# Splitting the dense weights once on TensorE, normalizing the gate and up input once, and taking GpSimd out of the dense part of a two-layer adaptive-norm MoE kernel

## The chip, the cores and the metric

The program runs on one core of a Trainium2 chip. The metric is the device time of one execution in microseconds. Three runs of the kernel before took 5500.07, 5501.99 and 5503.63 us, so the median is 5501.99 us.

## What is computed

The input x has 4 sequences of 1024 tokens with 1024 channels; a side input has the same shape; each sequence has a condition vector of 256 numbers. Two layers follow each other, and both begin with the same kind of bidirectional decayed scan over time:

```python
def _bi_wkv(r, k, v, w, u, time_emb):
    tf = sigmoid(sum(time_emb))
    decay = exp(-exp(w)) * (0.5 + 0.5 * tf)
    ek = exp(min(k, 30)); ekv = ek * v
    # nf, df: forward scans of ekv and ek; nb, db: backward scans
    euk = exp(min(u + k, 30))
    num = nf + nb - ekv + euk * v
    den = df + db - ek + euk
    return sigmoid(r) * (num / maximum(den, 1e-08)) * (0.8 + 0.2 * tf)

x = x + _L0_ffn_ref(_bi_wkv(x, side, side, ...))       # one 1024 x 1024 product, scale, bias
x = x + _L1_ffn_ref(_bi_wkv(x, side, side, ...))       # residual inside: RMS norm, then
#   routed: softmax over 32 experts, top 4, silu(h @ w1_gate) * (h @ w1_up) @ w2 for each
#   shared: silu(h @ sg) * (h @ su) @ sd, with sg, su, sd of 1024 x 1024
```

## The kernel before, in words

Matrix products run in fp32r on split operands: every operand is written as a high half (a rounded copy, ScalarE) and a low half (operand minus high half), and a product is three matmuls, high x high, high x low and low x high.

**Scan units.** The 4 x 8 channel blocks of 128 channels are 32 units (`unit(u, fill)` on each engine). In a unit VectorE computes both layers' scans of one block over 1024 tokens: four scans of a layer (L808, L812, L821, L829), each with a small edge factor (L810, L823), and a dozen elementwise operations of 128x1024. ScalarE supplies exponentials, logarithms (L574, L576) and the sigmoid of x. The results go to `gated_dram` and `ratio_dram`, and the side input and x of the next unit are loaded, all by the SyncE queue.

**Halves and steps.** The dense part works on 8 halves of 512 tokens (`HALVES`). A half has 32 steps. Each step is one `product`: 24 matmuls of 128x512 over one 128-column piece of 1024 weights rows (L1174). Steps 0 to 15 alternate between layer 0 (L products, `step_l`) and the down projection of the half before (D products, `step_d`); steps 16 to 31 alternate gate and up (`step_g`). Four PSUM banks hold products. In every step ScalarE makes the high half of the weight piece (L598) and GpSimd its low half (L212, `split_piece_lo`), with two slots for a piece, which SyncE loads two steps ahead (`load_piece`, 512 KB). The same pieces are split again in each of the 8 halves.

**Order of the work.** `with_halves` writes out the order on every engine. Units 0 to 6 run alone. Unit 7 carries the loading and splitting of the input of half 0, and each of the units 8 to 31 carries 8 steps: `fill(i)` calls stand at eight fixed places in a unit, so that four units go with a half (halves 0 to 5). Halves 6 and 7 run without units. All engines are in order, so a `fill` that waits holds up the unit behind it.

**Around the normalization.** For each of the 8 channel blocks o of a half VectorE computes `XL` (L1029), `C1` (L1015), `Z = C1 * norm_w` (L1022) and `RES` (L1037); ScalarE makes the sigmoid, the square `SQ` (L634) and the high half of Z (L632); GpSimd makes its low half (L245); TensorE's `by_token`, at step `step_l(o) + 2`, transposes Z for the rows that the experts will gather, accumulates the router logits (L1190) and the sum of squares (L1192). Gate and up are computed from the input that is not yet normalized. The factor R = 1/rms is known at step 17; it is applied afterwards to the gate (L981 on VectorE, `gate_scaled`), once more by GpSimd to the up side (`gate_r`, L218; `gate_silu`, L223), and to the logits. GpSimd also makes the low halves of the activations (L228) and of the layer input (L257).

**Routing and experts.** In half 7 VectorE ranks the experts (`route`, from step 21 on, ending with `entry_ready`, L960). GpSimd first fills `slots_dram` with empty entries (`empty_slots`, L493) and then puts 128 groups of entries there (`put_entries`, L472 to L477), SyncE reads them back, GpSimd gathers token rows, and the experts run: 32 experts, weights of 6 MB each (L1273, L1287). R of each token goes through the slots to the experts as a second column of `gains`.

Of the kernel before, what the change touches and what calls it, by code (L numbers as in the profile page):

```python
# [28 lines left out]
PIECES = 10  # L29

def step_l(o):
    return 0 if o == 0 else 2 * o - 1
# [15 lines left out]
def adaln_moe(nc, x_t, side_t, cond, w_all, u_all, lin_sb, norm_w, router_t, shared_w, expert_w, out):  # L50
# [8 lines left out]
    slots_dram = nc.dram_tensor("slots_dram", (SLOT_TILES * P, 4), i32).ap()  # L59

    ctx = ExitStack()
    with ctx:
# [3 lines left out]
        def sem(name):  # L66
# [5 lines left out]
        halves = sb("halves", 6 * OP + 4 * PIECE, f32r)  # L72
        chi, clo, zhi, zlo, ahi_s, alo_s = (halves[:, i * OP:(i + 1) * OP] for i in range(6))
        piece_hi, piece_lo = ([halves[:, 6 * OP + (2 * i + part) * PIECE:6 * OP + (2 * i + part + 1) * PIECE]
                               for i in range(2)] for part in range(2))
# [5 lines left out]
        SCAN = 9 * SEQ  # L81
        work = sb("work", SCAN + 2 * PIECE + OP + 13 * HALF)
        K, X, EK, EKV, W, F, G, H, N = (work[:, i * SEQ:(i + 1) * SEQ] for i in range(9))
        piece_in = [work[:, SCAN + i * PIECE:SCAN + (i + 1) * PIECE] for i in range(2)]
        RES = work[:, SCAN + 2 * PIECE:SCAN + 2 * PIECE + OP]
        part0 = SCAN + 2 * PIECE + OP
        XL0, XL1, C10, C11, RL, Z, SQ, ZS, RS, OV, R, T, SG = (
            work[:, part0 + i * HALF:part0 + (i + 1) * HALF] for i in range(13))
        XL, C1 = [XL0, XL1], [C10, C11]
# [6 lines left out]
        entry = work[:, part0:part0 + TT * TOPK * 4].bitcast(i32)  # L96
        where = work[:, part0 + HALF:part0 + HALF + TT * TOPK].bitcast(i32)
        slots = work[:, part0 + 2 * HALF:part0 + 2 * HALF + 4 * SLOT_TILES].bitcast(i32)


        RESET, LG, CAND, INCL = K, X, EK, H
# [6 lines left out]
        acc = sb("acc", TT * 33)  # L108
        rms = sb("rms", TT)

        GT = SLOT_TILES
        gains = acc[:, 0:2 * GT]
# [31 lines left out]
        for name in (  # L144
            "k_in x_in ramp consts_in cond_in kc ek ekv euk h_fwd h_edge h_bwd h_all den g_ln g_inv nf n_edge nb "
            "wv_done num newton1 newton2 sig_steps sig_x gated gated_raw ratio ratio_out gated_out "
            "piece_hi piece_lo product read_out rl_in cl_in c_hi c_lo sig1_steps sig1 c1 z sq z_hi z_lo res "
            "z_tr sums z_copy z_out mean r_ln r_exp newton_r r_set scaled l_tr l_acc silu_steps silu_sig g_r "
            "g_silu a_hi_s a_lo_s o_tr o_copy o_out prep prep_act masks rt rt_act rt_mask rt_pe cnt_copy "
# [11 lines left out]
        piece_sem = [sem(f"piece_in{i}") for i in range(2)]  # L161
# [11 lines left out]
        def wait(eng, name, value):  # L173

            if not (isinstance(value, int) and value <= 0):
                eng.wait_ge(s[name], value)

# [32 lines left out]
        def split_piece_lo(eng, h, k):  # L210
            eng.wait_ge(s["piece_hi"], h * STEPS + (k + 1))
            eng.tensor_tensor(piece_lo[k % 2], piece_in[k % 2], piece_hi[k % 2].bitcast(f32),  # L212
                               ALU.subtract).then_inc(s["piece_lo"], 1)

        def gate_r(eng, h, j):

            eng.wait_ge(s["silu_steps"], (h * CB + j) * 2 + 1)
            eng.tensor_tensor(T, T, R, ALU.mult).then_inc(s["g_r"], 1)  # L218

        def gate_silu(eng, h, j):  # L220
            eng.wait_ge(s["silu_sig"], h * CB + (j + 1))
            eng.wait_ge(s["g_r"], h * CB + (j + 1))
            eng.tensor_tensor(T, T, SG, ALU.mult).then_inc(s["g_silu"], 1)  # L223

        def split_act_lo(eng, h, j):
            eng.wait_ge(s["a_hi_s"], h * CB + (j + 1))
            part = slice(j * HALF, (j + 1) * HALF)
            eng.tensor_tensor(alo_s[:, part], OV, ahi_s[:, part].bitcast(f32), ALU.subtract).then_inc(s["a_lo_s"], 1)  # L228

        def low_halves(eng, h, i, first, prev, next_):  # L230


# [1133 lines left out]
```

## Time and profile before

| | us |
|---|---|
| median of 3 runs | 5501.99 |
| the profiled execution | 5515.08 |
| its span, first to last instruction | 5513.1 |
| TensorE busy in the span | 4469.8 |
| VectorE busy | 3139.4 |
| ScalarE busy | 1907.9 |
| GpSimd busy | 1923.7 |
| mean granted TensorE clock, share of full speed | 0.936 |

The span is cut by the program into three parts: units alone until about 360 us, dense steps until about 2600 us, and, after a stretch in which TensorE is idle, the experts. The busy share of an engine is to be read part by part.

### The profile page before, as it was taken

The numbers are of one execution on the slowest core, as the hardware profiler recorded it, in microseconds if no ns is written. First come the engines' busy times: TensorE is split into PE (matmuls) and PEld (weight loads), VectorE is DVE, ScalarE is ACT, GpSimd is POOL, SyncE is SP. The second block draws the span as 40 slices with busy tenths as digits, with TensorE's granted clock in tenths as the row PEclk, the third lists the DMA queues.
The fourth block names the chain that finished last, engine by engine and source line by source line (L and its number), as shares of the span: only waits on it lengthen the run. The fifth ranks groups of instructions, "written<-read, shape, count | busy, mean of one in ns | idle before, by whom it ended". The sixth has DMA issues, their size and how long they took to land.

```text
span 5513.1 us, 61940 instructions
## 1 busy us (share of the span) xinstructions
PE 4469.8 (81%) x19471; PEld 3552.8 (64%) x19473; DVE 3139.4 (57%) x2812; ACT 1907.9 (35%) x2587; POOL 1923.7 (35%) x1350
## 2 busy tenths in 40 slices
PE   0036786868777787997459999999999999999998
PEld 0014555655555565765348888878878887888887
DVE  8889898988989896445222323434343214324232
ACT  2234444434444444442212223333343214223232
POOL 0023748475656657554721111111111111111111
PEclk9998888989888888998779999999999999999999
DMA  1123342424333334345433444545564435445352
GB/s 59 53 84 99 108 137 106 145 96 134 109 125 113 116 118 136 119 132 75 135 82 104 107 107 117 180 123 175 151 194 148 107 61 175 122 105 149 89 163 57
DMA packets 248186, 649.34 MB, mean 118 GB/s; under 512 B 44720, under 2 KB 110704, under 8 KB 223472
## 3 DMA queue, kind: packets, MB, share of 16 engines
q1 hardware_dynamic: 200224, 489.21, 26.0%
q0 software_dynamic: 47824, 158.43, 13.9%
q8 instruction: 69, 1.13, 0.1%
q14 instruction: 69, 0.57, 0.0%
HBM read 500.69 MB, written 146.87 MB: 117 GB/s over the span
## 4 chain that ended last, share of the span: by engine, by line
PE 53%; issue 2%; POOL 2%; DVE 1%; DMA 1%; ACT 0%; DVEq 0%; POOLq 0%; ACTq 0%; SPq 0%
PE ps L1273 30%; PE ps L1287 15%; PE ps L1174 4%; PE ps L1254 2%; POOL slots_dram L477 2%; PE ps L1262 1%; DMA slots_dram<-work 1%; PE ps L1192 0%; PE ps L1190 0%; DMA work<-slots_dram 0%; POOL halves L212 0%; DVE work L890 0%; DVE work L887 0%; DVE work L886 0%; POOL work L223 0%
## 5 line engine op out<-in xcount | busy, mean ns | idle before, releaser
L1174 PE MATMUL ps<-halves 128*128 128x512 f32 x6144 | 1606.3, 424 | 713.0 <-POOL halves L257 352.3
L1174 PEld LDWEIGHTS ps<-halves 128*128 128x128 f32 x6144 | 1249.5, 205 | 1066.7 <-issue 439.1
L1273 PE MATMUL ps<-halves 128*128 128x512 f32 x7152 | 1745.6, 397 | 27.5 <-DVE halves L1102 22.1
L1273 PEld LDWEIGHTS ps<-halves 128*128 128x128 f32 x7152 | 1328.9, 189 | 300.9 <-DVE halves L1102 24.3
L212 POOL TENSOR_TENSOR halves<-work,halves 128x1024 fp32r<-128x1024 f32 x239 | 694.9, 2909 | 675.7 <-ACT halves L598 675.4
L1287 PE MATMUL ps<-halves 128*128 128x512 f32 x3576 | 835.0, 389 | 1.3 <-DVE halves L1112 1.3
L1287 PEld LDWEIGHTS ps<-halves 128*128 128x128 f32 x3576 | 671.4, 188 | 140.5 <-DVE halves L1112 1.5
L1097 DVE TENSOR_TENSOR halves<-ps,halves 128x1024 fp32r<-128x1024 f32 x150 | 183.7, 1225 | 876.1 <-ACT halves L696 876.1
L459 POOL COPY add_idx<-work 128x1 int32 x149 | 27.0, 181 | 1692.1 <-DVE work L1118 1692.1
L1102 DVE TENSOR_TENSOR halves<-work,halves 128x1024 fp32r<-128x1024 f32 (+1 forms) x320 | 440.3, 1435 | 109.8 <-ACT halves L705 109.8
L696 ACT ACTIVATE halves<-ps 128x1024 fp32r<-128x1024 f32 x150 | 153.9, 1026 | 960.7 <-PE ps L1273 849.3
L705 ACT ACTIVATE halves<-work 128x1024 fp32r<-128x1024 f32 (+1 forms) x320 | 369.4, 1220 | 97.7 <-PE ps L1287 65.7
L598 ACT ACTIVATE halves<-work 128x1024 fp32r<-128x1024 f32 x256 | 268.3, 1048 | 271.8 <-PE ps L1174 167.2
L1107 DVE SCALAR_TENSOR_TENSOR work<-ps,acc,work 128x256 f32<-128x256 f32 x298 | 142.7, 479 | 285.1 <-ACT work L711 285.1
L462 POOL DMA_INDIRECT out<-work,add_idx x149 | 240.1, 1611 | 129.7 <-POOL add_idx L459 126.1
L1254 PE MATMUL ps<-ident,work 128*128 128x128 f32 x1200 | 156.2, 273 | 135.2 <-DMA work<-rows_dram,row_idx 135.2
L1118 DVE TENSOR_SCALAR work<-ps,acc 128x512 f32<-128x512 f32 x149 | 111.6, 749 | 266.1 <-PE ps L1287 259.5
L711 ACT ACTIVATE work<-ps,acc 128x256 f32<-128x256 f32 x298 | 140.2, 470 | 330.3 <-PE ps L1273 330.3
L257 POOL TENSOR_TENSOR halves<-work,halves 128x512 fp32r<-128x512 f32 x64 | 128.2, 2004 | 355.4 <-ACT halves L661 355.4
L1254 PEld LDWEIGHTS ps<-ident,work 128*128 128x128 f32 x1200 | 140.5, 140 | 154.7 <-DMA work<-rows_dram,row_idx 135.4
L1112 DVE TENSOR_TENSOR halves<-ps,halves 128x256 fp32r<-128x256 f32 x298 | 112.2, 419 | 220.2 <-ACT halves L716 220.2
L722 ACT ACTIVATE work<-ps,acc 128x512 f32<-128x512 f32 x149 | 101.3, 680 | 386.4 <-PE ps L1287 379.2
(163 smaller groups left out, 4582.0 us busy)
## 6 DMA issues: line engine op xcount, KB each, us to landing
work<-expert_w SPq DMA_DIRECT2D x192, 1024.0 KB, 5.5
work<-shared_w SPq DMA_DIRECT2D x256, 512.0 KB, 4.4
work<-side_t SPq DMA_DIRECT2D x33, 512.0 KB, 3.4
work<-x_t SPq DMA_DIRECT2D x33, 512.0 KB, 4.1
gated_dram<-work SPq DMA_DIRECT2D x32, 512.0 KB, 3.0
ratio_dram<-work SPq DMA_DIRECT2D x32, 512.0 KB, 2.9
work<-gated_dram SPq DMA_DIRECT2D x64, 256.0 KB, 2.7
work<-x_t SPq DMA_DIRECT2D x64, 256.0 KB, 3.2
```

Source lines behind the costliest of these rows:

```text
L212: eng.tensor_tensor(piece_lo[k % 2], piece_in[k % 2], piece_hi[k % 2].bitcast(f32), ALU.subtract).then_inc(s["piece_lo"], 1)
L462: pool.indirect_dma_start(out[:, :], bass.IndirectOffsetOnAxis(add_idx[:, :].bitcast(u32), 0), y, None, compute_op=ALU.add).then_inc(s["y_ ...
L598: sc.activation(piece_hi[k % 2], piece_in[k % 2], ACT.Copy).then_inc(s["piece_hi"], 1)
L696: sc.activation(xhi, ps_xt[:, :], ACT.Copy).then_inc(s["x_hi"], 1)
L705: sc.activation(whi[:, part], stage[:, part], ACT.Copy).then_inc(s["w_hi"], 1)
L1097: ve.tensor_tensor(xlo, ps_xt[:, :], xhi.bitcast(f32), ALU.subtract).then_inc(s["x_lo"], 1)
L1102: ve.tensor_tensor(wlo[:, part], stage[:, part], whi[:, part].bitcast(f32), ALU.subtract).then_inc(s["w_lo"], 1)
L1107: ve.scalar_tensor_tensor(part, ps_h[:, a * 512 + 256:a * 512 + 512], gains[:, ds(g + GT, 1)], part, ALU.mult, ALU.mult).then_inc(s["act_d ...
L1174: last = pe.matmul(bank(k % 4), w[k % 2][:, c * P:(c + 1) * P], op[:, part], start=(c == 0 and w is piece_hi and op is hi), stop=(c == CB ...
L1254: last = pe.transpose(ps_xt[:, c * P:(c + 1) * P], hx[:, c * P:(c + 1) * P], ident[:, :])
L1273: last = pe.matmul(ps_h[:, a * 512:a * 512 + 512], xp[:, xk * P:(xk + 1) * P], wp[:, rhs], start=(xk == 0 and xp is xhi and wp is whi), st ...
L1287: last = pe.matmul(ps_y[:, h * 512:h * 512 + 512], ap_[:, (q * 2 + k) * P:(q * 2 + k + 1) * P], wp[:, rhs:rhs + 512], start=(q == 0 and k ...
```

## The change

It is a set of edits that belong together.

1. **Weights are split once.** During the 8 first units, each of the 32 weight pieces is loaded into one of four raw buffers, ScalarE makes the high half, TensorE subtracts (identity times raw, plus negative identity times high, in fp32, into PSUM), ScalarE copies the difference as the low half, and SyncE stores both halves (1 MB) to `split_dram`. For the eighth unit's four pieces this is done ahead of the unit.
2. **Pieces are loaded already split.** A step loads 1 MB in two chunks of 512 KB, three steps ahead, in four slots. ScalarE's L598 and GpSimd's L212 are gone from the steps.
3. **The input of gate and up is normalized once**, in a burst at step 16. C1 of all 8 blocks is kept; Z = C1 * norm_w * R comes at step 16, block by block, with its two halves, transposes and logits. The sums of squares stay in the steps, at `step_l(o) + 1`. `gate_scaled`, `gate_r` and `gate_silu` become one VectorE multiply with the sigmoid; R no longer goes to the experts.
4. **GpSimd's remaining low halves move to VectorE** (8 for the layer input, 8 for Z, 8 for the activations in a half).
5. **In a unit** the two edge factors of a layer move from VectorE to ScalarE, both forward scans come first, and four operations change the buffer that they write.
6. Token rows are stored to `rows_dram` once a half (2 MB) and no longer block by block.
7. GpSimd waits for the last RES only before it fills `slots_dram`.

```diff
+        def alone(u, i):                       # SyncE
+            m = i // 2
+            if i % 2 == 0:
+                sp.wait_ge(s["split_pe"], u * 4 + (m + 1))
+                sp.dma_start(raw_w[m], shared_w[ds((u * 4 + m) * P, P), :]).then_inc(raw_sem[m], 16)
+            else:
+                sp.wait_ge(s["split_lo"], u * 4 + (m + 3))
+                sp.dma_start(split_dram[...], split_w[m]...).then_inc(split_sem[m], 16)
+        def alone(u, i):                       # ScalarE
+            m = i // 2
+            if i % 2 == 0:
+                sc.wait_ge(raw_sem[m], (u + 1) * 16)
+                sc.wait_ge(split_sem[m], u * 16 + 1)
+                sc.activation(split_part(m, 0), raw_w[m]..., ACT.Copy).then_inc(s["split_hi"], 1)
+            else:
+                sc.wait_ge(s["split_pe"], u * 4 + (m + 5))
+                sc.activation(split_part(m, 1), ps[m % 2]..., ACT.Copy).then_inc(s["split_lo"], 1)
+        with pe.Fori(0, 2 * UNITS_PER_HALF) as u:          # TensorE
+            for m in range(4):
+                pe.wait_ge(s["split_hi"], u * 4 + (m + 1))
+                pe.wait_ge(s["split_lo"], u * 4 + (m + 1))
+                for j in range(2):
+                    pe.matmul(ps[m % 2][:, part], ident[:, :], raw_w[m][:, part], start=True, stop=False)
+                    last = pe.matmul(ps[m % 2][:, part], neg_ident, split_w[m]..., start=False, stop=True)
+                last.then_inc(s["split_pe"], 1)
-            nothing = lambda i: None
             with eng.Fori(0, 2 * UNITS_PER_HALF - 1) as u:
-                unit(u, nothing, alone=True)
+                unit(u, lambda i: alone(u, i))
+            last = 2 * UNITS_PER_HALF - 1
+            for i in range(FILLS_PER_UNIT):
+                alone(last, i)
+            weights()
...
-                pe.wait_ge(s["piece_lo"], h * STEPS + (k + 1))
+                for j in range(2):
+                    pe.wait_ge(piece_sem[k % SLOTS][j], arrived(h, k))
...
-                    if i == step_l(o) + 2:
-                        by_token(h, o)
+                    if i == step_l(o) + 1:
+                        square_sums(h, o)
+                if i == 2 * CB - 1:
+                    for o in range(CB):
+                        by_token(h, o)
+                if i == 2 * CB:
+                    logits_by_token(h)
...
+        def normalize(h):                      # VectorE, at step 16
+            ve.tensor_scalar(SQ, SUM_BANK, 1.0 / CH, 1e-6, ALU.mult, ALU.add)
+            ve.wait_ge(s["r_exp"], h + 1)
+            ve.scalar_tensor_tensor(SG, R, -0.5, R, ALU.mult, ALU.mult)
+            ve.tensor_tensor(SG, SG, SQ, ALU.mult)
+            ve.scalar_tensor_tensor(R, SG, 1.5, R, ALU.add, ALU.mult)
+            for o in range(CB):
+                if o < 2:
+                    wait(ve, "l_tr", h)
+                else:
+                    ve.wait_ge(s["z_lo"], h * CB + (o - 1))
+                    ve.wait_ge(s["logits"], h * CB + (o - 1))
+                ve.scalar_tensor_tensor(Z[o % 2], C1[o], nrm[:, o:o + 1], R, ALU.mult, ALU.mult)
+                if o:
+                    split_z_lo(h, o - 1)
+            split_z_lo(h, CB - 1)
...
                     ve.tensor_tensor_scan(F, d, EK, 0.0, ALU.mult, ALU.add).then_inc(s["h_fwd"], 1)
+                    ve.tensor_tensor_scan(G, d, EKV, 0.0, ALU.mult, ALU.add).then_inc(s["nf"], 1)
-                    ve.tensor_scalar(edge_in[:, 0:1], F[:, SEQ - 1:SEQ], edge[:, at], None, ALU.mult)
-                    ve.tensor_tensor_scan(H[:, ::-1], d, F[:, ::-1], edge_in[:, 0:1], ALU.mult, ALU.add)
+                    ve.tensor_tensor_scan(F[:, ::-1], d, F[:, ::-1], edge_in[:, 0:1], ALU.mult, ALU.add)
```

## Rows read from the trace of the kernel before

**Rows 1.** The page: busy tenths in 40 equal slices of the span.
```profile
DVE  8889898988989896445222323434343214324232
...
POOL 0023748475656657554721111111111111111111
```

**Rows 2.** Windows: stretch, then length, PE, PEld, DVE, ACT, POOL busy (x count), PEclk, DMA share, GB/s.
```profile
811.00:973.00 162.00, 110.27 (x389) 85.43 (x388) 143.51 (x86) 67.73 (x86) 125.55 (x48) 0.82 0.28 99
973.00:1113.00 140.00, 118.63 (x481) 84.39 (x480) 127.68 (x95) 64.08 (x85) 63.67 (x24) 0.96 0.44 142
...
2811.00:5513.00 2702.00, 2657.65 (x12524) 2205.40 (x12522) 951.64 (x1205) 827.77 (x1206) 444.89 (x598) 0.99 0.45 128
```

**Rows 3.** VectorE's groups in 30 to 330 us, units alone, GpSimd idle.
```profile
L808 DVE TENSOR_TENSOR_SCAN work<-decay,work 128x1024 f32<-128x1024 f32 x14 | 32.0, 2284 | 0.0
...
L847 DVE SCALAR_TENSOR_TENSOR work<-work,neg_gain 128x1024 f32<-128x1024 f32 x14 | 18.0, 1284 | 1.1
```

**Rows 4.** VectorE's groups in 440 to 2050 us, units with steps, GpSimd busy.
```profile
L808 DVE TENSOR_TENSOR_SCAN work<-decay,work 128x1024 f32<-128x1024 f32 x43 | 127.9, 2976 | 0.0
L847 DVE SCALAR_TENSOR_TENSOR work<-work,neg_gain 128x1024 f32<-128x1024 f32 x43 | 121.3, 2822 | 5.2 <-DVE work L844 2.5
...
L991 DVE TENSOR_TENSOR work<-ps,work 128x512 f32<-128x512 f32 x41 | 28.1, 686 | 40.9 <-POOL work L223 40.9
```

**Rows 5.** VectorE's timeline: start, duration, line; two unit starts, an edge factor's place.
```profile
59.93 1.22 DVE L802 TENSOR_TENSOR work<-work 128x1024 f32<-128x1024 f32 x1
...
80.97 2.28 DVE L808 TENSOR_TENSOR_SCAN work<-decay,work 128x1024 f32<-128x1024 f32 x1
...
83.63 2.35 DVE L812 TENSOR_TENSOR_SCAN work<-decay,edge_in,work 128x1024 f32<-128x1024 f32 x1
...
102.18 1.22 DVE L802 TENSOR_TENSOR work<-work 128x1024 f32<-128x1024 f32 x1
```

**Rows 6.** VectorE's timeline: the start of unit 8 and the last operation of unit 31.
```profile
362.53 2.29 DVE L802 TENSOR_TENSOR work<-work 128x1024 f32<-128x1024 f32 x1
...
2151.51 2.19 DVE L847 SCALAR_TENSOR_TENSOR work<-work,neg_gain 128x1024 f32<-128x1024 f32 x1
```

**Rows 7.** TensorE's timeline: fp32 matmuls after an idle stretch and in dense work.
```profile
425.32 1.92 PE L1190 MATMUL ps<-work,rw 128*32 128x512 f32 x2
427.16 2.08 PE L1192 MATMUL ps<-work,ones 128*128 128x512 f32 x2
...
2181.73 1.05 PE L1190 MATMUL ps<-work,rw 128*32 128x512 f32 x2
2182.71 1.13 PE L1192 MATMUL ps<-work,ones 128*128 128x512 f32 x2
```

**Rows 8.** The chain that ended last: start, duration; two pairs of products in half 6.
```profile
2197.67 10.93 PE ps L1174 x48
2211.50 10.93 PE ps L1174 x48
```

**Rows 9.** DMA issues in 20 to 300 us: count, KB each, median us to landing.
```profile
work<-x_t SPq DMA_DIRECT2D x7, 512.0 KB, 3.8
work<-side_t SPq DMA_DIRECT2D x6, 512.0 KB, 3.3
```

**Rows 10.** ScalarE's groups over the span: a 128x1024 copy, a 128x512 square.
```profile
L598 ACT ACTIVATE halves<-work 128x1024 fp32r<-128x1024 f32 x256 | 268.3, 1048 | 271.8 <-PE ps L1174 167.2 <-DMA work<-shared_w 99.4 <-issue 5.2
...
L634 ACT ACTIVATE work<-work 128x512 f32<-128x512 f32 x64 | 39.3, 614 | 0.0
```

**Rows 11.** Timeline: the mean of squares in halves 6 and 7, `entry_ready`, the first put.
```profile
2267.93 0.68 DVE L1041 TENSOR_SCALAR work<-ps 128x512 f32<-128x512 f32 x1
...
2495.14 0.68 DVE L1041 TENSOR_SCALAR work<-ps 128x512 f32<-128x512 f32 x1
...
2564.70 0.09 DVE L960 MEMSET work<- 128x32 f32 x1
...
2588.68 0.18 POOL L472 COPY put_idx<-work 128x4 int32<-128x4 int32 x1 [26.79 <-DMA slots_dram<-work]
```

More of the change, by code:

```diff
@@ L29 @@
 PIECES = 10
+SLOTS = 4
+AHEAD = SLOTS - 1
 def step_l(o):
@@ L379, in store_out, with unit @@
                 sp.dma_start(to, RS.rearrange("p (t c) -> p t c", c=P)).then_inc(s["o_out"], 16)
-            def unit(u, fill, alone=False):
+            def unit(u, fill):
                 fill(0)
@@ L407, in _ @@
             load_x(0)
-            for k, src in first_half[:2]:
-                load_piece(0, k, src)
-            with_halves(sp, unit, fill, tail)
+            with_halves(sp, unit, fill, tail, alone, weights)
             def load_weights(j):
@@ L502, in fill @@
                     pool.dma_start(out[TOK:TOK + P, :], K).then_inc(s["y_out"], 16)
[L503 to L512 removed]
+            fill(HALVES - 2, 2, first=False, prev=True, next_=True)
+            fill(HALVES - 1, FIRST_RANK + 1, first=False, prev=True, next_=False)
             pool.wait_ge(s["entry_ready"], 1)
@@ L793, in clip, with unit @@
                 ve.tensor_scalar(EK, K, 30.0, None, ALU.min).then_inc(s["kc"], 1)
-            def unit(u, fill, alone=False):
+            def unit(u, fill):
                 fill(0)
@@ L1164, in product @@
+            pe.wait_ge(s["split_lo"], 2 * UNITS_PER_HALF * 4 + 2)
             def product(h, k, hi, lo, ready, at):
-                pe.wait_ge(s["piece_lo"], h * STEPS + (k + 1))
                 wait(pe, "read_out", h * STEPS + (k - 3))
-                for c in range(CB):
-                    if ready:
-                        pe.wait_ge(s[ready], at + (c + 1))
-                    part = slice(c * HALF, (c + 1) * HALF)
-                    for w, op in ((piece_hi, hi), (piece_hi, lo), (piece_lo, hi)):
-                        last = pe.matmul(bank(k % 4), w[k % 2][:, c * P:(c + 1) * P], op[:, part],
-                                         start=(c == 0 and w is piece_hi and op is hi), stop=(c == CB - 1 and w is piece_lo))
@@ L1176, in product @@
-                last.then_inc(s["product"], 1)
+                for j in range(2):
+                    pe.wait_ge(piece_sem[k % SLOTS][j], arrived(h, k))
+                    chunk = piece[k % SLOTS][j]
+                    for c in range(CB // 2 * j, CB // 2 * (j + 1)):
+                        if ready:
+                            pe.wait_ge(s[ready], at + (c + 1))
+                        part = slice(c * HALF, (c + 1) * HALF)
+                        col = c % (CB // 2) * P
+                        w_hi, w_lo = chunk[:, col:col + P], chunk[:, HALF + col:HALF + col + P]
+                        for w, op in ((w_hi, hi), (w_hi, lo), (w_lo, hi)):
+                            last = pe.matmul(bank(k % 4), w, op[:, part],
+                                             start=(c == 0 and w is w_hi and op is hi), stop=(c == CB - 1 and w is w_lo))
+                    last.then_inc(s["chunk" if j == 0 else "product"], 1)
@@ L1178, in by_token, with square_sums @@
+            def square_sums(h, o):
+                pe.wait_ge(s["sq"], h * CB + (o + 1))
+                if o == 0:
+                    wait(pe, "mean", h)
+                pe.matmul(SUM_BANK, ones[:, :], SQ, start=(o == 0), stop=(o == CB - 1)).then_inc(s["sums"], 1)
             def by_token(h, o):
```

532 lines of the change are left out of this document (258 added, 274 removed).

## The prediction, made before the changed kernel was run

> **What bounds the kernel now.** I read the page's slices first, then busy time by stretch, then VectorE's groups with and without GpSimd beside them, then the timelines. The slices [rows 1] show VectorE at 8 or 9 tenths until slice 15 or so, about 2100 us, and idle for the most part after. So the first 2150 us are VectorE's. From 2811 us on TensorE is busy 2657.7 of 2702 us [rows 2]; nothing in the change shortens that stage (the gate-up multiply loses a factor, but TensorE does not wait for it).
>
> The finding on which most hangs is that VectorE is not busy because it has so much to do. With GpSimd idle a forward scan takes 2.28 us, the last multiply 1.28 [rows 3]; with GpSimd busy the same lines take 2.98 and 2.82 [rows 4]. An operation that reads PSUM for one operand stays at 0.69 beside GpSimd [rows 4]. So what is slowed is work with both operands in SBUF, and GpSimd is what differs. Four units and 32 steps take 302 us in this stretch (162 + 140), of which VectorE is busy 271 [rows 2].
>
> **Part 1, the split during the units alone: a cost.** A unit alone takes 42.25 us (59.93 to 102.18 [rows 5]). The new work is a chain, and it is serial. SyncE is in order: it loads raw piece m, then waits for the low half of m before it stores it, and only then loads m + 1. Four raw buffers do not help. So every piece costs load, ScalarE copy, four fp32 matmuls, ScalarE copy.
> - Load: 512 KB alone lands in 3.3 us; x, issued right behind a 512 KB store, lands in 3.8 [rows 9]; with half a microsecond for the issue of the store, an estimate, 1 MB takes 4.3: so 2.3 us and 2 us per MB. In the same queue the four loads stand behind the 1 MB store of the last piece, and three of them also behind the unit's own transfers: 1.5, 2, 2.5 and 2 MB to be moved, so 5.3, 6.3, 7.3, 6.3: 25 us. Lower bound 3.3 each, upper 8.
> - Copies: 1.05 each [rows 10], two.
> - TensorE: one fp32 matmul of 512 columns takes 1.84 us start to start after an idle stretch (425.32 to 427.16) and 0.98 in dense work [rows 7]. The granted clock is at the lower of its two levels in the former, at the upper in the latter. TensorE idles some 8 us between pieces here, so I take the lower level for most: 6.3 us for four, between 3.9 and 7.4.
> - Hand-overs, four: 0.6 together, an estimate.
>
> A piece is then 9.0 us and its load, a unit 25 + 36 = 61 us, against VectorE's own 40.7, which is hidden in it. (VectorE's own: 42.25 less the edge factors, which take 83.63 - 80.97 - 2.28 = 0.38 us each, four of them [rows 5].) The Trainium skill, "DMA: Bandwidth & Descriptors", section on the anatomy of one DMA, puts a transfer at about 2.0 us and 436 GB/s. By it the four loads would take some 27 us, and the whole stage would be about 16 us longer; no run here shows a 1 MB store in front of a load.
>
> Seven units: 16 + 7 x 61 - 7 (the first has no store ahead) = 436. The eighth unit's pieces are split before it, with ScalarE and SyncE blocked, so VectorE waits: 4 x (5.3 + 9.0) = 57, until 493. Then SyncE waits for the last store (4.3), and issues six chunk loads ahead of the first layer input, which stands first in ScalarE's and VectorE's unit: 3.25 MB, 9 us; then its halves 1.4. Unit 7 starts at about 508 and takes 38.7 and 7 lows of 0.69: unit 8 starts at 552. Before: 362.5 [rows 6]. **Cost: 190 us.** Bounds: by the lower ends a unit is 44 us and the cost 60; by the upper ends (8 and 7.4) 72 us and 280.
>
> **Part 2, halves 0 to 5: the gain.** They take 362.5 to 2154 us, 1791, or 298.5 each. VectorE's work for a half without GpSimd: four units of 42.25 - 2 (the wait for the side input, hidden by steps here) - 1.5 = 38.7 make 155. Per block it now has ten operations of 0.69 (XL, C1, RES, down, Z, two gate multiplies, three lows): 55. With R's steps, 213. TensorE needs 32 x 5.47 [rows 8] and fp32 and transposes, about 206. Neither can be the time, because the new order ties them:
> - `square_sums(o)` stands one step earlier than `by_token` did. TensorE has just finished D, VectorE must add down (0.69), make C1 (0.69), ScalarE the square (0.61 [rows 10]) before the sum (1.0) and the next two products (10.9) and transposes (0.5): 14.7 us for a pair with hand-overs. VectorE's stretch between is longer in every other pair (two scans more): some 16.6 and 17.8. Steps 1 to 15 make 110 us.
> - At step 16 TensorE waits for everything: newton's start comes after down and RES, mean, two ScalarE operations, three on VectorE: Z0 is there 15 us after the last pair began; then 8 blocks of transposes and logits, with one PSUM bank for the transposes and two Z buffers: some 2.2 us each, and the first of them at the lower clock. 35 us in all, of which VectorE works 15.
> - Steps 16 to 31: VectorE has two units, 77.4, 15 or so multiplies and activation lows, 8 input lows (20.6 with them), stalls 4: 102. TensorE has 88 and is hidden. The next half's first stretch is 9.6.
>
> A half is 257 us. Half 0 has no D products: 235. Sum 1520. **Gain: 271 us.** Bounds for a half: 240, if the wait at each pair is hidden by the units, and 275, if every hand-over costs half a microsecond more. Weights come at 1 MB a step; three steps ahead is 16 us against some 5, so I cost it at nothing. If that cover is gone (SyncE held by a store that waits for VectorE), TensorE is late next.
>
> **Part 3, halves 6 and 7.** Between their means 227.2 us pass [rows 11]. A pair took 13.83 [rows 8], and 14.7 now, plus the burst of step 16, less the by-token work taken out of the pairs; in steps 16 to 31 GpSimd no longer slows anything: 230. Cost 3.
>
> **Part 4, routing.** From half 7's mean to the first put 93.6 us pass; 24 of them after `entry_ready`, waiting for the fill of `slots_dram` [rows 11]. Now the fill starts with the last RES, ahead of the burst and not after step 21, which is more than those 24 us earlier, so the puts start at `entry_ready`. From mean to `entry_ready` 69.6 us pass [rows 11]. The burst now stands in between: 24 us from mean to product 16, where before TensorE was in its products within 4; the copies of R that are gone give back 2.5. So 87. Gain 7.
>
> Sum: 190 - 271 + 3 - 7 = -85. Profiled execution 5515.1 - 85 = 5430; the median stands 13 us below that execution, so **5417 us**.
>
> **Costed at nothing.** The edge factors on ScalarE: the second forward scan and the backward one (2.3 us each) cover them and the exponential behind them; without that cover VectorE waits some 1 us in each layer. The logarithms now write the buffer whose store they wait for; that store was issued a scan or more earlier. Rows stored once a half (2 MB) instead of 8 times: SyncE issues 7 fewer, and the only ones who wait are ScalarE's first layer-input half at step 24, 15 us and more behind, and the gathers. The experts' silu without its scale: TensorE is busy 98% there [rows 2]. GpSimd's added mask: TensorE waits for it only at the start.
>
> **Rivals.**
> 1. *The split hides better*: TensorE stays at its upper clock and transfers overlap, 44 us a unit. For it: the queue's 2 MB are not one block. Against: SyncE's order. Then 130 us less: 5287. Chance 0.12.
> 2. *The lockstep eats the gain; slower.* Place: the pairs of steps 1 to 15 and the burst. In order engines wait for each other twice a pair, and each of four engines can be late with unit work. It decides from 257 + 85 / 6 = 271 us a half on. At 275 to 280, 1660 us for part 2: 5547. For it: VectorE idles 30 us a half even now. Against: a quarter of that is waiting for GpSimd (40.9 us at L991 alone in 5.4 halves [rows 4]). Chance 0.22.
> 3. *VectorE stays slow*, the slowing being due to transfers or ScalarE. Then nothing is gained in part 2, and the time is 5417 + 271 = 5688. ScalarE and transfers run beside the units alone too, at the undisturbed durations [rows 3]. Chance 0.03.
>
> **How the numbers follow.** The forecast keeps 0.63. The range takes in its unknowns: half of the way to both bounds in parts 1 and 2. 5310 reaches close to rival 1, 5550 holds most of rival 2. No change is within 0.2%, 11 us, about what a measurement of this kernel can tell. The forecast's 0.63 is 0.57 faster and 0.06 same; with rival 1 faster has 0.69. Of the 0.25 of rivals 2 and 3, 0.02 end within the bound: slower 0.23, same 0.08.
>
> **What would show it.** Unit starts in the first stage 61 us apart, VectorE waiting there for ScalarE, and ScalarE for the raw loads and TensorE. Unit 8 at about 550. Forward scans at 2.28 us, the last multiply at 1.28 in every part, GpSimd idle till the slots. Halves of 257 us, TensorE waiting for the square at each pair and about 6 us at step 16. Wrong if units alone stay near 42 us, or if halves are over 271 us.

## The result, and the profile after

The changed kernel takes **5607.46 us** (median; 5604.76 to 5610.94), the kernel before, beside it on the same chip, 5502.81. The ratio is 1.0191, with a 95% interval of 1.0173 to 1.0209: **1.9% slower**. The prediction of 5417 us, range 5310 to 5550, was wrong, and in its sign. The span went from 5513.1 to 5606.3 us, and these 93 us can be laid out by the events that the prediction used (starts and ends from VectorE's and GpSimd's timelines; the rows of before are [rows 6, 11]):

| stretch | before | after | difference | predicted |
|---|---|---|---|---|
| start to unit 8 (L802, now L832) | 362.5 | 573.8 | +211 | +190 |
| units 8 to 31, halves 0 to 5 | 1791 | 1679 | -112 | -271 |
| end of unit 31 to the mean of half 6 | 114 | 123 | +9 | 0 |
| mean of half 6 to mean of half 7 | 227.2 | 229.2 | +2 | +3 |
| mean of half 7 to the first put | 93.5 | 84.4 | -9 | -7 |
| first put to the end | 2924.4 | 2917.5 | -7 | 0 |

One row is wrong by 159 us, and the sign hangs on it. The windows of the changed kernel, cut at the stages (length, then busy us and count of TensorE, its weight loads, VectorE, ScalarE and GpSimd; granted clock, DMA share, GB/s):

```profile
16.00:444.00 428.00, 159.78 (x216) 61.56 (x216) 257.96 (x172) 129.16 (x149) 0.00 (x0) 0.67 0.37 132
444.00:574.00 130.00, 43.23 (x71) 20.14 (x72) 45.75 (x38) 29.51 (x35) 0.00 (x0) 0.62 0.32 113
574.00:2256.00 1682.00, 1292.70 (x4998) 966.24 (x4997) 1213.09 (x1103) 636.51 (x922) 0.76 (x1) 0.87 0.53 182
2256.00:2604.00 348.00, 302.91 (x1254) 231.92 (x1252) 106.63 (x147) 86.33 (x138) 0.00 (x0) 0.95 0.64 196
...
2905.00:5606.00 2701.00, 2656.30 (x12524) 2203.34 (x12524) 933.71 (x1205) 801.21 (x1206) 446.31 (x598) 0.99 0.45 128
```

The expert stage is as it was (2701 us, [rows 2] had 2702). In the dense part GpSimd is empty, and VectorE is now busy 1213 us of 1682, 72%, where the 302 us of [rows 2] had 90%. So the work did shrink. No engine is full: TensorE has 77%, and it is granted 0.87 of its clock. VectorE's groups in 900 to 2100 us show that the shrinking came as forecast:

```profile
L838 DVE TENSOR_TENSOR_SCAN work<-decay,work 128x1024 f32<-128x1024 f32 x34 | 77.6, 2283 | 0.0
L870 DVE SCALAR_TENSOR_TENSOR work<-work,neg_gain 128x1024 f32<-128x1024 f32 x34 | 43.7, 1285 | 2.8
```

These are the durations of [rows 3]; beside GpSimd they had been 2976 and 2822 ns [rows 4]. What is new is in the waits of the same stretch, 4.2 halves (us in total, times, longest):

```profile
PE ps L1223 <- ACT work L664: 151.0, 35, 13.9
...
DVE work L1078 <- PE ps L1215: 110.1, 28, 6.0
DVE halves L1025 <- ACT halves L697: 91.8, 32, 7.5
...
DVE work L1034 <- PE ps L1215: 64.9, 18, 7.2
```

L1223 is the matmul of `square_sums`; it waits for ScalarE's square of the block, at every block. L1025 is `split_c_lo`, the low half of the next layer input, now VectorE's. And VectorE waits for TensorE's products (L1215) while TensorE waits for it: a lockstep. TensorE's timeline (start, duration, line, idle before) shows one whole pair of it:

```profile
1447.68 1.54 PE L1223 MATMUL ps<-work,ones 128*128 128x512 f32 x2 [3.50 <-ACT work L664]
1448.24 7.66 PE L1215 MATMUL ps<-halves 128*128 128x512 f32 x24
1455.74 0.60 PE L1249 MATMUL ps<-ident,work 128*128 128x128 f32 x4
1456.10 5.74 PE L1215 MATMUL ps<-halves 128*128 128x512 f32 x24
1464.03 1.13 PE L1223 MATMUL ps<-work,ones 128*128 128x512 f32 x2 [2.20 <-ACT work L664]
```

Two things are to be seen. The wait: 2.20 us here, 2.04 or 2.20 in 20 of the 40 places between 700 and 2110 us, and 3.5 us or more in the others. And the product behind it: the same 24 matmuls take 7.66 us there and 5.74 in the second place. The windows over the product behind the second of these waits (it began at 1464.59 and took 7.66 us again) say why:

```profile
1466.00:1468.00 2.00, 2.00 (x6) 1.61 (x5) 1.96 (x2) 0.00 (x0) 0.00 (x0) 0.50 1.07 379
...
1470.00:1472.00 2.00, 2.00 (x10) 1.64 (x9) 0.00 (x0) 0.00 (x0) 0.00 (x0) 1.00 0.90 262
```

In the wait of 2.20 us that ends at 1464 the granted clock is still 1.00 (1462 to 1464 us); from 1466 on it stands at 0.50, the lower of its two levels, and it is back at 1.00 when this product nears its end. It is not so each time: of the 20 such products behind a wait of 2.0 to 2.2 us, 8 took 6.03 to 6.06 us and 12 took 7.03 to 7.67; the 20 behind a wait of 3.5 us or more took 6.99 to 8.45. So most waits cost themselves and some 1.6 us more.

The first pair of a half has the longest wait:

```profile
1396.26 8.36 PE L1215 MATMUL ps<-halves 128*128 128x512 f32 x27 [6.29 <-DVE halves L1025]
1418.48 2.07 PE L1223 MATMUL ps<-work,ones 128*128 128x512 f32 x2 [13.86 <-ACT work L664]
1419.56 8.30 PE L1215 MATMUL ps<-halves 128*128 128x512 f32 x24
```

ScalarE's sigmoid of block 0 stood behind the exponential and the sigmoid of a unit (it began at 1414.02), and VectorE's C1 behind a scan (at 1417.09).

### The profile page after: what moved, and what is told of

It reads as the page before. It is cut to its first block, busy times and chain, and to the rows that moved or that the text cites. A ratio compares the mean times of both kernels' runs of the same rounds, so it can differ in the third digit from the quotient of the medians.

```text
span 5606.3 us, 61272 instructions
## 1 busy us (share of the span) xinstructions
PE 4612.6 (82%) x19727; PEld 3603.9 (64%) x19729; DVE 2648.6 (47%) x2813; ACT 1737.9 (31%) x2531; POOL 599.8 (11%) x811
## 3 DMA queue, kind: packets, MB, share of 16 engines
q0 software_dynamic: 47824, 158.43, 13.5%
## 4 chain that ended last, share of the span: by engine, by line
PE 66%; DVE 12%; issue 8%; DMA 6%; ACT 5%; POOL 2%; SPq 1%; DVEq 0%; POOLq 0%; ACTq 0%
PE ps L1320 29%; PE ps L1334 14%; PE ps L1215 13%; DMA plain<-shared_w 3%; PE ps L1301 2%; PE ps L1223 2%; POOL slots_dram L494 1%; DMA work<-gated_dram 1%; PE ps L1195 1%; DVE work L853 1%; DVE work L838 1%; PE ps L1309 1%; DVE work L841 1%; DVE work L844 1%; PE ps L1196 1%
## 5 line engine op out<-in xcount | busy, mean ns | idle before, releaser
L1215 PE MATMUL ps<-halves 128*128 128x512 f32 x6144 | 1579.4, 418 | 165.9 <-DVE halves L1025 83.6
L1215 PEld LDWEIGHTS ps<-halves 128*128 128x128 f32 x6144 | 1229.4, 202 | 495.8 <-issue 151.9
L1195 PE MATMUL ps<-plain,ident 128*128 128x512 f32 x128 | 112.3, 975 | 321.1 <-ACT halves L626 321.1
L1223 PE MATMUL ps<-work,ones 128*128 128x512 f32 x128 | 99.2, 866 | 267.0 <-ACT work L664 267.0
L1195 PEld LDWEIGHTS ps<-plain,ident 128*128 128x128 f32 x128 | 35.5, 308 | 378.3 <-ACT halves L626 347.9
L1134 DVE TENSOR_TENSOR work<-ps,work 128x256 f32<-128x256 f32 x298 | 124.9, 419 | 240.9 <-ACT work L742 240.1
L1223 PEld LDWEIGHTS ps<-work,ones 128*128 128x128 f32 x128 | 24.2, 236 | 294.9 <-ACT work L664 294.8
```

The source lines that it names most:

```text
L1134: ve.tensor_tensor(part, ps_h[:, a * 512 + 256:a * 512 + 512], part, ALU.mult).then_inc(s["act_done"], 1)
L1195: pe.matmul(ps[m % 2][:, part], ident[:, :], raw_w[m][:, part], start=True, stop=False)
L1215: last = pe.matmul(bank(k % 4), w, op[:, part], start=(c == 0 and w is w_hi and op is hi), stop=(c == CB - 1 and w is w_lo))
L1223: pe.matmul(SUM_BANK, ones[:, :], SQ, start=(o == 0), stop=(o == CB - 1)).then_inc(s["sums"], 1)
```

## The experiments

The theory after these readings: the change lost by its order, in three places. (a) TensorE waits for each block's square, and loses clock by it. (b) VectorE waits for the upper halves of the input, where GpSimd used to wait. (c) The split is a chain of hand-overs, in which each load waits for the store of the piece before. The general rival: units and products set the pace anyway, and the waits only show it.

Each kernel ran with the kernel before beside it (medians of 5501.9 to 5510.1 us), and the ratio is to that.

| kernel | median, us | ratio to before, 95% interval | a half, us |
|---|---|---|---|
| changed | 5607.5 | 1.0173 to 1.0209 | 283.1 |
| e1 | 5348.8 | 0.9701 to 0.9733 | 246.4 |
| e2 | 5515.9 | 1.0014 to 1.0033 | 266.5 |
| e3 | 5436.5 | 0.9864 to 0.9897 | 282.4 |
| e4 | 5683.3 (one run) | | 306.0 with GpSimd busy |
| e5 | 5563.8 | 1.0093 to 1.0126 | 275.5 |
| e6 | 5496.6 | 0.9980 to 0.9999 | 265.1 |
| c1 | 5075.3 | 0.9195 to 0.9225 | 228.7 |
| c2 | 5046.0, again 5045.1 | 0.9158 to 0.9183 (the second) | 228.8 |
| c3 | 5021.9 | 0.9113 to 0.9138 | 227.2 |

A half is the distance from the mean of half 0 to that of half 5 (L1039 in VectorE's timeline), divided by five.

### e1: the square one product later

```diff
-                        if i == step_l(o) + 1:
+                        if i == step_l(o) + 2:
                             square_sums(h, o)
```

> Only the matmul that adds up the squares of a block moves, one product later in TensorE's order (the old order). Theory (lockstep): in the changed kernel TensorE waits 35 times, 151 us in 4.2 halves, for the square of the block that VectorE has only just finished, and after each such wait the granted clock drops and the next product takes 7.66 us and not 5.72. With the square one product later the square is 5 us old when TensorE comes to it: the waits of TensorE at L1223 go from 151 us to under 15, the products of the pairs are all near 5.7 us, a pair falls from 17.4 to 13.5 us, a half from 284 to 258 us (250 to 268) and the kernel from 5607 to about 5455 us (5400 to 5510), below the kernel before. Rival (VectorE and the work of the units are the bound anyway, TensorE's wait only shows their pace): the wait moves to another line, a half loses under 5 us, and the kernel stays above 5575 us.

Measured: 5348.8 us, 259 less than the changed kernel and 2.8% under the kernel before. The gain is larger than the theory's range. TensorE's timeline in e1:

```profile
1592.35 0.60 PE L1249 MATMUL ps<-ident,work 128*128 128x128 f32 x4
1592.79 1.02 PE L1223 MATMUL ps<-work,ones 128*128 128x512 f32 x2
1593.25 11.46 PE L1215 MATMUL ps<-halves 128*128 128x512 f32 x48
1604.55 0.60 PE L1249 MATMUL ps<-ident,work 128*128 128x128 f32 x4
1604.98 1.02 PE L1223 MATMUL ps<-work,ones 128*128 128x512 f32 x2
1605.44 11.47 PE L1215 MATMUL ps<-halves 128*128 128x512 f32 x48
```

A pair is 12.2 us (1592.79 to 1604.98), with no idle time in it and both products at 5.73. In the changed kernel the pair above took 16.35 (1447.68 to 1464.03), and those with the longer waits up to 19.9. The theory had 13.5. The waits at the squares in 900 to 2100 us, and what TensorE waits for now:

```profile
PE ps L1215 <- DVE work L1004: 62.5, 11, 7.8
PE ps L1233 <- DVE work L1055: 31.6, 5, 6.7
PE ps L1223 <- ACT work L664: 28.8, 9, 5.3
```

28.8 us are left, not under 15: at the first pair of a half and at one or two others. Of the five short ones between 690 and 1910 us, those of 1.31, 1.62 and 1.66 us left the two products behind them at 11.49 us; behind those of 1.73 and 1.74 us the granted clock fell to 0.50 again, and the two products took 12.98 and 13.06. The stretch without units gained as well: from the mean of half 6 to that of half 7 207.9 us pass and not 229.2, so it is not unit work alone that makes the square late. The rival is refuted: a VectorE that set the pace would have kept it.

### e5: useless matmuls in the wait

The square stays at its early place, and TensorE has something to do before it:

```diff
...
+                for n in range(9):
+                    pe.matmul(Z_BANK, chi[:, 0:P], chi[:, 0:HALF], start=True, stop=True)
                 pe.wait_ge(s["sq"], h * CB + (o + 1))
```

The lines left out let TensorE wait, before the first block, until the bank that the useless products write is free.

> The changed kernel, but before each wait for a square TensorE does nine matmuls of 128x128 by 128x512 in the halves' type, whose result nobody reads (nine of the 24 of a product of 5.74 us: 2.15 us of work, as long as its shortest waits). The square stays where it is. Theory (the lockstep costs twice: 2.2 to 3.5 us of wait, and then a product at a lower granted clock, 7.66 and not 5.74 us): with TensorE busy in the wait the first product of a pair takes 5.7 to 6.2 us, a pair falls from 17.4 to about 15.6 us, a half loses 9 to 14 us although TensorE has 17 us more to do in it, and the kernel comes to 5515 to 5560 us. Rival 1 (the clock falls for another reason, or the longer product is only what the wait's end makes of it): the first product stays at 7.66 us, the kernel within 5595 to 5620 us. Rival 2 (the added matmuls lie on the path): the kernel is slower, 5640 to 5720 us.

Measured: 5563.8 us. With 17.6 us more work for TensorE in each half (nine matmuls in 2.20 us, eight times), the kernel is 44 us **faster**. The timeline:

```profile
1475.18 2.20 PE L1224 MATMUL ps<-halves 128*128 128x512 f32 x9
1477.55 1.13 PE L1228 MATMUL ps<-work,ones 128*128 128x512 f32 x2 [0.16 <-ACT work L664]
1478.11 6.03 PE L1215 MATMUL ps<-halves 128*128 128x512 f32 x24
...
1460.25 2.07 PE L1228 MATMUL ps<-work,ones 128*128 128x512 f32 x2 [3.71 <-ACT work L664]
1461.34 8.11 PE L1215 MATMUL ps<-halves 128*128 128x512 f32 x24
```

Where the filling leaves 1.5 us of wait or less, all 30 first products take 6.02 to 6.06 us (granted clock 1.00 in 1478 to 1484 us); where it leaves 3.7 us or more, all ten take 6.95 to 8.32 (0.50 in 1461 to 1465 us). So the clock's part is real and separate: the square comes by the same path, and only what TensorE did meanwhile differs. A half lost 7.6 us, under the theory's 9 to 14, and the kernel missed the range by 4 us; the ten longer waits are those that outlast the filling. Of the 36.7 us a half that e1 wins, at least these 7.6 are the clock.

### e2 and e6: who waits for the input halves

e2 moves `load_cl` ahead of `next_piece` (and the loads of the first two of the eight blocks a step earlier), and puts ScalarE's copy first in the step:

```diff
+                if next_:
+                    for c in range(CB):
+                        if i == STEPS - CB + (c - 1 if c > 1 else 0 if before_all(h) else -1):
+                            load_cl(h + 1, c)
                 if not before_all(h) and any(i == a for a, _ in products(h, first)):
...
-                        if i == STEPS - CB + max(c - 1, 0):
-                            load_cl(h + 1, c)
```

> SyncE issues the four loads of the next half's input a step earlier and ahead of that step's weight piece, and ScalarE makes the upper halves of that input as the first thing of their step. Theory: VectorE, which now makes the lower halves itself and in order, waits 92 us in 4.2 halves (22 us a half) at L1025 for those upper halves, because the load stands behind a piece of weights and the copy behind the activation's. With both earlier the wait falls to under 30 us in 4.2 halves, a half loses 8 to 16 us, and the kernel comes to 5510 to 5560 us. Rival (those waits lie beside TensorE's products of the upper steps and cost nothing): the wait at L1025 falls as much, VectorE waits for TensorE at the next line instead, a half loses under 3 us, and the kernel stays within 5585 to 5610 us.

e6 leaves loads and copies where they are and gives the subtraction back to GpSimd:

```diff
-                            split_c_lo(h + 1, c)
...
+            def split_c_lo(h, c):
+                pool.wait_ge(s["c_hi"], h * CB + (c + 1))
+                part = slice(c * HALF, (c + 1) * HALF)
+                pool.tensor_tensor(clo[:, part], RL[c % 2], chi[:, part].bitcast(f32), ALU.subtract).then_inc(s["c_lo"], 1)
```

> The changed kernel with one of its moved parts undone: the lower halves of the input of gate and up (eight subtractions of 128x512 a half) are made by GpSimd again, which waits for the upper halves instead of VectorE. Theory (what e2 won, 92 us, is the wait of VectorE, in order, and not the earlier load as such): VectorE's wait at that line, 92 us in 4.2 halves, is gone, and although eight operations of GpSimd in a half read SBUF beside VectorE and take 2.2 us each instead of 0.69, the kernel comes to 5510 to 5560 us. Rival (TensorE needs those halves as late as before and is the one that waits, or the slower subtraction is on its path): TensorE's wait for the lower halves at the first product of a half grows by over 8 us, and the kernel stays above 5585 us.

Measured: e2 5515.9 us, 92 less than the changed kernel, inside the theory's range. e6 5496.6 us, 111 less, 13 us better than its range. VectorE's wait at L1025 in 900 to 2100 us of e2 (91.8 us in 32 times in the changed kernel; ScalarE's copy now stands at L661), and GpSimd's group in e6:

```profile
DVE halves L1025 <- ACT halves L661: 26.6, 8, 5.0
```

```profile
L524 POOL TENSOR_TENSOR halves<-work,halves 128x512 fp32r<-128x512 f32 x34 | 55.1, 1620 | 1235.1 <-ACT halves L707 1235.1
```

Two unlike edits, an earlier supply and another waiter, take 16.5 and 17.9 us from a half. What they share is that VectorE no longer stands still: the wait was on the path. (e6 also spares VectorE the eight subtractions, 8 x 0.69 = 5.5 us a half, so it would prove less alone; in e2 VectorE still does them.) GpSimd's subtraction took 1.62 us, not the 2.2 that I had from the old kernel's rows. Its 1235 us of waiting cost nothing.

### e3: the raw loads ahead

```diff
-                if i % 2 == 0:
-                    sp.wait_ge(s["split_pe"], u * 4 + (m + 1))
-                    sp.dma_start(raw_w[m], shared_w[ds((u * 4 + m) * P, P), :]).then_inc(raw_sem[m], 16)
+                if i == 0:
+                    for r in range(4):
+                        sp.wait_ge(s["split_pe"], u * 4 + (r + 1))
+                        sp.dma_start(raw_w[r], shared_w[ds((u * 4 + r) * P, P), :]).then_inc(raw_sem[r], 16)
```

> In the first seven units, and in the eighth unit's split, SyncE issues the four loads of raw weights at the first step and not each before its own store. Theory (the split is a chain of hand-overs: load, upper half, TensorE, lower half, store, and only then the next load): with the loads ahead, a unit falls from 61.5 to 46 us (44 to 50), and the kernel from 5607 to about 5495 us (5470 to 5525). Rival 1 (the split is bound by its operations: TensorE in fp32 at the lower clock and ScalarE's copies): a unit stays above 57 us and the kernel above 5575 us. Rival 2 (the DMA engines are the bound): the landing of a raw load gets longer than 9 us and the unit stays above 55 us.

Measured: 5436.5 us, 171 less, and past the theory's range. The units alone are 41 us apart (220.23 to 261.25) and not 62; unit 8 starts at 397.8 and not at 573.8. So VectorE's own 40.7 us bind, as in the kernel before. The chain in the changed kernel, one piece of it (the timeline in 91 to 102 us):

```profile
91.71 0.40 SPq L412 DMA_DIRECT2D split_dram<-halves  x1
92.36 0.35 SPq L409 DMA_DIRECT2D plain<-shared_w  x1
...
97.91 1.06 ACT L626 ACTIVATE halves<-plain 128x1024 fp32r<-128x1024 f32 x1 [6.37 <-DMA plain<-shared_w]
98.87 1.04 ACT L600 ACTIVATE work<-work 128x1024 f32<-128x1024 f32 x1
...
101.09 1.23 DVE L866 TENSOR_TENSOR work<-work 128x1024 f32<-128x1024 f32 x1 [7.49 <-ACT work L602]
```

The load leaves 0.6 us after the store, and ScalarE stands 6.4 us for it, in order, with the unit's own L600 and L602 behind it; VectorE waits 7.5 us for L602. ScalarE's waits for the raw loads, in 16 to 444 us of the changed kernel and in 16 to 300 us of e3:

```profile
ACT halves L626 <- DMA plain<-shared_w: 194.5, 26, 9.3
```

```profile
ACT halves L627 <- DMA plain<-shared_w: 45.1, 6, 8.2
```

Both rivals are refuted: TensorE at 0.76 of its clock (16 to 300 us) and the copies fit into 41 us; the DMA share could rise from 0.37 to 0.54 in the same stretch, and a raw load lands in 5.6 us (median), where it took 5.7 in 16 to 444 us of the changed kernel.

### e4: GpSimd reads SBUF for nothing

```diff
+            with pool.Fori(0, 800) as n:
+                pool.wait_ge(s["pulse"], n + 1)
+                pool.tensor_tensor(idle_out[:, :], rw[:, :], rw[:, :], ALU.add).then_inc(s["pulse"], 1)
```

> GpSimd, idle in the changed kernel, does 801 additions of 128x256 fp32 in SBUF (the result is used by nothing) one after the other, beginning in the third half. Theory (VectorE became faster because GpSimd left SBUF): in the stretch with the additions VectorE's scans of 128x1024 go from 2.28 back to 2.5 to 3.0 us and its multiplications of the units from 1.28 to over 1.8 us, the operations that read PSUM (0.69 us) stay, and the halves of that stretch take 20 to 60 us more. Rival (VectorE became faster because its own operands and order changed): the scans stay within 2.25 to 2.35 us beside the additions, and the halves stay at 284 us.

Measured: one run, 5683.3 us; the three halves with the additions take 306.0 us, the two before them 284.1, 22 more each. VectorE's groups in 1300 to 2100 us, in e4 and then the same lines in the changed kernel:

```profile
L845 DVE TENSOR_TENSOR_SCAN work<-decay,work 128x1024 f32<-128x1024 f32 x21 | 54.2, 2583 | 0.0
L855 DVE SCALAR_TENSOR_TENSOR work<-work,cap 128x1024 f32<-128x1024 f32 x21 | 33.6, 1601 | 0.4 <-DVE work L851 0.4
L1022 DVE TENSOR_TENSOR halves<-work,halves 128x512 fp32r<-128x512 f32 x24 | 25.6, 1065 | 0.0
L1041 DVE TENSOR_TENSOR work<-ps,work 128x512 f32<-128x512 f32 x19 | 12.9, 679 | 35.9 <-PE ps L1222 33.6 <-PE ps L1256 2.3
```

```profile
L838 DVE TENSOR_TENSOR_SCAN work<-decay,work 128x1024 f32<-128x1024 f32 x23 | 52.5, 2283 | 0.0
L848 DVE SCALAR_TENSOR_TENSOR work<-work,cap 128x1024 f32<-128x1024 f32 x23 | 29.4, 1278 | 0.4 <-DVE work L844 0.4
L1015 DVE TENSOR_TENSOR halves<-work,halves 128x512 fp32r<-128x512 f32 x23 | 15.5, 676 | 0.0
L1034 DVE TENSOR_TENSOR work<-ps,work 128x512 f32<-128x512 f32 x23 | 15.7, 681 | 49.8 <-PE ps L1215 44.1 <-PE ps L1249 5.7
```

A scan goes from 2283 to 2583 ns, a multiply from 1278 to 1601, a subtraction in SBUF from 676 to 1065, and the addition that reads PSUM stays (681, 679). That is the pattern of [rows 3, 4]; the multiplies did not reach the 1.8 us that I gave. It shows that GpSimd's leaving made VectorE faster. The Trainium skill, "SBUF — State Buffer", section "Who interferes with whom", says that a VectorE instruction with two SBUF inputs contends with a GpSimd instruction that reads SBUF, and one with at most one SBUF input, outside VectorE's two-port modes, does not. These rows agree: 1601 for 1278 ns, and 679 for 681. Not every operation with one SBUF input was spared: the `tensor_scalar` of 128x1024 at L823 (L830 in e4) went from 689 to 1047 ns. In which mode it ran no view shows.

### c1, c2, c3: together

c1 has the edits of e1, e2 and e3.

> The three edits of e1, e2 and e3 together. Theory (three separate losses: the square that TensorE waits for, the input halves that VectorE waits for, the chain of hand-overs in the split): the gains add up, since the split lies before the halves (171 us) and the two waits lie in different steps of a half (259 us, and 92 us alone): 5607 - 259 - 171 - 92 = 5085 us, 5075 to 5125. Rival (the waits at the input halves only take up slack that TensorE's order leaves, and once the square is out of the way TensorE itself is the bound): e2 adds nothing on top, and the kernel stays above 5160 us.

c2 also does the eighth unit's split beside that unit:

```diff
-            for i in range(FILLS_PER_UNIT):
-                alone(last, i)
-            weights()
-            unit(2 * UNITS_PER_HALF - 1, lambda i: fill(-1, STEPS - FILLS_PER_UNIT + i, first=False, prev=False, next_=True))
+            def both(i):
+                alone(last, i)
+                fill(-1, STEPS - FILLS_PER_UNIT + i, first=False, prev=False, next_=True)
+            unit(last, both)
+            weights()
```

> As c1, and the split that stands alone between the seventh and the eighth unit (VectorE idles some 74 us there in the changed kernel, 48 of them more than a unit with its split takes) is done beside the eighth unit's own arithmetic. Theory: the eighth unit with both ends 41 to 50 us after it begins, where the split alone (about 41) and the unit (48) stood one behind the other: 30 to 45 us less than c1. Rival (the first weight pieces of the first half, which may only be loaded after the whole split, now come too late): at least 25 of these us come back as a wait of TensorE for its first piece, and c2 is within 20 us of c1.

c3 is c2 with the low halves of the input on GpSimd, as in e6; c2 ran again beside it.

> c2 with the lower halves of the input made by GpSimd, as in e6. Theory: in c2 TensorE is the bound of the halves (it idles only some 24 us in a half of 229 us, and 17 us in 4.3 halves at the first product, behind VectorE's lower halves), so what e6 won in the changed kernel is not to be had again: 0 to 5 us a half, 5010 to 5050 us. Rival (VectorE's work and waits still set the half): another 12 us a half or more, under 4975 us. Second rival (GpSimd's 2.2 us subtractions, beside which VectorE's operations take up to 1.3 times as long, now lie on the path): slower than c2, over 5055 us.

> c2 once more beside c3, on the same chip, so that the two can be compared: 5035 to 5055 us.

Measured: c1 5075.3 us. The three gains, 258.7 + 91.6 + 171.0, from 5607.5 would give 5086.2, 11 us more than measured: the losses were separate, and the rival of c1 is refuted. c2 took 29 us less than c1, one under its range; unit 8 starts at 366.7 us and not at 406.0, and 8 of these 39 us are lost again before the mean of half 0 (467.5 for 499.0). c3 came out at 5021.9, 23 us under c2, inside the theory's range: its mean of half 0 stands at 457.9 and not 467.5, and a half is 1.5 us shorter. So the fastest version takes **0.913 of the time of the kernel before** (0.9113 to 0.9138). Its window in 600 to 1600 us, with columns as above:

```profile
600.00:1600.00 1000.00, 906.51 (x3817) 696.84 (x3815) 887.51 (x781) 467.77 (x675) 56.27 (x32) 0.96 0.67 233
```

TensorE is busy 91% and VectorE 89%, where the changed kernel's dense stage had 77 and 72, and the granted clock is 0.96 and not 0.87.

## Why the prediction was wrong, by its steps

**Part 1, the split.** Forecast +190 us, measured +211, within its bounds. The named cause, a serial chain in SyncE's order, was right: e3 breaks it and gets 41 us. A unit takes 62.9 (75.34 to 389.78, five of them), forecast 61, and VectorE runs out of work at 451.7, forecast 436; it then waits 73.6 us for the eighth unit's split, forecast 72; and unit 7 takes 47.9, forecast 44. These make the 21 us. What was too small is a piece without its load: the one from 438.90 to 454.85 us takes 15.95 us, 5.75 of them the load, so 10.2 where the sum had 9.0. The loads were rather too dear in the sum, 25 us for four against a median landing of 5.7 each. The Trainium skill's figure that stands beside them ("DMA: Bandwidth & Descriptors", "Anatomy of one DMA — SWDGE (gpsimd) path") is one for GpSimd's path and not for SyncE's queue; the 27 us that it gave are farther off still. And the lower bound of 44 us for a unit does not follow from its own ends: 4 x (3.3 + 2.1 + 3.9 + 0.6) is 39.6, so VectorE's 40.7 would have been the floor, which is what e3 came to.

**Part 2, the term that failed.** Forecast 257 us a half and a gain of 271; measured 283.1 and 112. Even the upper bound of 275 was too low. By place, the mean of four halves from one product 16 to the next (in the changed kernel 716.48 to 1848.94 us), in us:

| place | forecast | changed | e1 | e2 | e5 | c1 |
|---|---|---|---|---|---|---|
| product 16 to VectorE's last low half of the input (steps 16 to 31) | 102 | 115.1 | 115.1 | 97.9 | 115.4 | 98.0 |
| then to the sum of the second square (9.6 and one pair of 15.7, the mean of 110 / 7) | 25.3 | 33.6 | 31.1 | 33.7 | 33.2 | 31.7 |
| then six pairs, to the sum of the last square | 94.3 | 103.9 | 76.1 | 104.2 | 96.5 | 74.8 |
| then to product 16 | 35 | 30.6 | 24.1 | 30.4 | 30.3 | 24.2 |

Two terms failed, and they share the excess of 26.6 us: 13.1 lie in the first place, 8.3 and 9.6 in the pairs, and -4.4 in the burst of Z. e2 acts on the first place alone, e1 on the others.

- *Steps 16 to 31.* The failed words are "stalls 4". One half of the changed kernel, in windows:

```profile
1280.01:1395.50 115.49, 98.24 (x414) 79.70 (x413) 86.29 (x74) 46.83 (x68) 0.00 (x0) 0.93 0.59 208
1395.50:1418.48 22.98, 8.36 (x28) 6.45 (x28) 20.84 (x19) 9.17 (x13) 0.00 (x0) 0.65 0.60 218
```

  VectorE computes 86.3 us here, where the sum had 98, and stands still for 29.2, where it had 4; L1025 alone is 22.8 of them. I had counted what VectorE computes and not what it must stand for now that it is GpSimd's heir. Without that wait (e2) the place takes 97.9 us, under the forecast.
- *The first pair.* It had no wait in the sum; TensorE waits 13.9 us for the first square. VectorE is busy for 20.8 of the 23.0 us before it (the second window): the 12 us of work that the sum had put into steps 16 to 31 are about what comes on top here. No experiment shortens this place by more than 3 us, so what could is open.
- *The other six pairs* were put at 14.7 to 17.8 us and take 17.3 on average, some 19.9. I saw the lockstep, and sized it by an undisturbed TensorE, 10.9 us for two products; with the lower clock they are up to 14.2 (8.45 and 5.74 from 1518.26 on). e5, which keeps the clock up in most of them, has 16.1.
- *The burst* of Z was a little too dear: 6.5 us of wait and 17 for eight blocks.

Either term alone would have left the kernel near the one before: 6 x 13.1 us bring the forecast to 5496, 6 x 17.9 to 5524. Without e1's and e2's losses a half is 228.7 us (c1), 54 less than in the changed kernel and under the lower bound of 240. The forecast had half of these 54 in it, most of them as the lockstep.

**What was right.** VectorE at its undisturbed durations (rival 3 refuted, by e4 too); halves 6 to 7, 229.2 for 230; routing 84.4 for 87, the first put 0.16 us behind `entry_ready`. Weight pieces made TensorE wait 0.6 us in all in 900 to 2100 us. The expert stage did not move.

**The rival that came true** is the second: the kernel is slower, and a half is beyond its point of 271 us. It had 0.22. At its place, the pairs and the burst, stands about half of the excess (8.3 + 9.6 - 4.4 = 13.5 of 26.6 us). The other half it did not have: the second wait, VectorE's at L1025. I had argued against it with a wait for GpSimd that would go; it went, and two new ones of 151 and 92 us in 4.2 halves came for it. (Its 5547 us do not follow from its own 1660: 5417 + 1660 - 1520 is 5557.)

## What to carry to other kernels

When an edit lets one engine read a result a step sooner, ask for the age of that result when it is read: a TensorE that arrives 2 us early in every pair pays twice, once in the wait and once in the clock. When work is moved from an idle engine to the one that sets the pace, count not only its duration but each wait that stands in front of it, for the idle engine could stand there for nothing. And where one queue both loads and stores a ring of buffers, issue the loads ahead of the store that waits; the number of buffers alone gives no overlap.

## What was unexpected of the hardware

Waits as short as 2.0 to 2.2 us were enough, in 12 cases of 20, for the granted clock to be at its lower level in the next product, which then took up to 7.67 us for 6.03; in e1 two waits of 1.73 and 1.74 us were enough. Behind 1.5 us or less it never was, in the 30 cases of e5. A kernel got 44 us faster by 17.6 us more of matmuls in each half. And GpSimd's subtractions of 128x512 took 1.62 us where it does only these, against the 2.1 to 2.3 us that they had in the kernel before, with GpSimd busy throughout; no run here tells why.
